# First attention: who counts the scores above the 32nd, ScalarE's sign pass or GpSimd's clamp with TensorE's row products

## What is computed

```python
scores = jnp.einsum('bthd,bghd->bhtg', Q, K) / np.sqrt(DH)     # 16 x 4 x 256 x 1601
topv, topi = jax.lax.top_k(scores, K_TOP)                       # K_TOP = 32
probs = jax.nn.softmax(topv, axis=-1)
attn = jnp.zeros_like(scores).at[bi, hi, ti, topi].set(probs)
c_t = jnp.einsum('btg,bgd->btd', attn.mean(axis=1), V)
```

## Time and profile before

| what | value |
|---|---|
| runs | 2945.46, 2946.61, 2954.35 us (median 2946.61) |
| span of the profiled execution | 2943.0 us, 3.6 us under the median run |
| first attention, from the first keep to the last | 1019.03 us, 127 slot intervals |
| one batch in the middle of it | 64.88 us, 8 slots |
| busy share in that batch | ACT 89%, PE 84%, DVE 82%, POOL 77% |

### The profile page before, as it was taken

How to read it: one execution, slowest core, us unless ns; L and a number is a source line. 1 busy time by engine, 2 the same in 40 slices (tenths; PEclk the granted TensorE clock), 3 DMA queues, 4 the chain that set the end, 5 groups by cost and what they waited for, 6 DMA issues and landing times. The chain is left out here.

```text
span 2943.0 us, 61087 instructions
## 1 busy us (share of the span) xinstructions
PE 2435.4 (83%) x19797; PEld 1266.0 (43%) x19797; DVE 2219.5 (75%) x8233; ACT 2102.0 (71%) x3547; POOL 1247.5 (42%) x1593
## 2 busy tenths in 40 slices
PE   7958888888888888668786589999999999999638
PEld 5735555555555555535422123333333333333337
DVE  8739878887887888446555989999999999994313
ACT  5759889888898988614322078888888888889325
POOL 1438777777777777613100502232222222200154
PEclk9979899989988998889898599999999999999669
DMA  8820000000000000091430224444344334330222
GB/s 241 266 76 12 13 15 13 14 13 13 17 20 13 15 13 13 8 308 36 60 118 32 79 43 100 101 102 101 90 95 101 87 92 94 94 64 2 59 92 67
DMA packets 163461, 205.77 MB, mean 70 GB/s; under 512 B 78588, under 2 KB 131106, under 8 KB 163126
## 3 DMA queue, kind: packets, MB, share of 16 engines
q1 hardware_dynamic: 152774, 161.80, 21.9%
q0 software_dynamic: 10352, 39.92, 4.0%
HBM read 135.19 MB, written 66.60 MB: 69 GB/s over the span
## 5 line engine op out<-in xcount | busy, mean ns | idle before, releaser
L2143 ACT ACTIVATE pb<-sps 128x512 f32<-128x512 f32 (+1 forms) x1664 | 891.9, 597 | 232.8 <-PE sps L2085 224.8
L2166 DVE TENSOR_REDUCE mx<-wps 128x2 f32<-128x802 f32 x1024 | 949.6, 988 | 49.8 <-PE wps L2058 35.0
L1076 DVE MAX8 cand<-sc 128x8 f32<-128x46 f32 (+1 forms) x4480 | 604.0, 199 | 138.3 <-issue 78.2
L2100 PE MATMUL ops<-pb,va 128*9 128x256 f32 x6656 | 516.4, 382 | 11.0 <-ACT ot L2149 7.2
L852 PE MATMUL scores<-ctxT,qT 97*128 97x512 f32 (+1 forms) x1024 | 437.2, 576 | 80.5 <-ACT sc L964 69.5
L852 PEld LDWEIGHTS scores<-ctxT,qT 97*128 97x128 f32 x1024 | 206.6, 212 | 318.4 <-issue 218.5
L1942 POOL COPY va<-XX 128x128 f32<-128x128 f32 (+1 forms) x208 | 49.9, 292 | 661.0 <-PE ops L2100 653.2
L735 POOL TENSOR_TENSOR prf<-sc,prf 128x1601 f32<-128x1601 f32 x64 | 229.7, 3589 | 127.0 <-ACT prf L971 127.0
L827 PE MATMUL misc<-diag,prs 128*128 128x128 f32 (+1 forms) x1664 | 238.0, 300 | 7.0 <-issue 6.1
L735 POOL TENSOR_TENSOR prs<-sc,prs 128x1601 f32<-128x1601 f32 x64 | 230.7, 3604 | 16.8 <-ACT prs L971 13.9
L2058 PE MATMUL wps<-FO,Y 56*128 56x401 bf16 x1024 | 187.8, 357 | 51.3 <-DVE mx L2166 36.4
(11 more groups left out here) (406 smaller groups left out, 3914.2 us busy)
## 6 DMA issues: line engine op xcount, KB each, us to landing
FO<-keys SPq DMA_DIRECT2D x392, 50.0 KB
XX<-keys SPq DMA_DIRECT2D x392, 50.0 KB
ctxn<-in_ctx_dram SPq DMA_DIRECT2D x32, 576.0 KB
keys<-kpb POOLq DMA_DIRECT2D x42, 400.2 KB, 3.7
toep<-kernpad SPq DMA_DIRECT2D x8, 2048.0 KB, 14.9
values<-s_vs SPq DMA_DIRECT2D x16, 832.0 KB, 6.0
XX<-values SPq DMA_DIRECT2D x16, 832.0 KB, 4.9
keysf<-s_kf SPq DMA_DIRECT2D x16, 800.5 KB, 3.8
```

Source lines behind the costliest of these rows:

```text
L1076: st.add(v.max(cand[s % 2][:, 8 + n:8 + n + 7 * NP + 1:NP], sc[s % 4][:, c:c + w]))
L2100: ins = t.matmul(ops[VW * i:VW * i + DH1 + 1, 0:S], va[par][0:kn(kt), kt, 4 * g + i, :], pb[(UNITS * g + 2 * kt + i % 2) % 8][0:kn(kt), i ...
L2143: nc.scalar.activation(pb[(UNITS * g + u) % 8][0:rows_, :, :], sps[(UNITS * g + u) % SB][0:rows_, :, :], ACT.Exp).then_inc(p_ready, 1)
L2166: v.tensor_reduce(mx4[:, q, h:h + 2, c], both, AX.X, ALU.max).then_inc(work_read, 1)
```

## The change

The sign pass leaves ACT, and `below32_of` leaves POOL. `keep_of` on POOL gets a clamp in front of the subtraction: the huge values in `pr` become 1 and the kept ones stay 0, written as bf16 to `side`. PE multiplies `side` with a column of -1 in four products of up to 401 columns into one row of PSUM, and adds the expected count with a fifth product. ACT sums that row of 401 into `doubts` (float; DVE loads its bits as an integer, positive where the float is positive).

```diff
+        COUNTED = -(-NK // 4)
-            st.link(g.memset(onecol[:, :], 1.0))
-            st.link(g.memset(plain[:, :], float(NK - 2 * TOPK)))
+            st.link(g.memset(onecol[:, :], -1.0))
+            st.link(g.memset(plain[0:P // 2, :], -3136.0))
+            st.link(g.memset(plain[P // 2:P, :], -(2.0 * (NK - TOPK) - 3136.0)))
...
-            def below32_of(s, j):
-
-                if not isinstance(j, int) or j >= 2:
-                    pool.wait_ge(sides_ready, j - 1)
-                pool.sem_inc(pool_passed, 1)
-                t32, e = top[:, s % 4, TOPK - 1:TOPK], slack[:, s % 2:s % 2 + 1]
-                st.link(g.tensor_scalar(e, t32, -1.0, t32, ALU.mult, ALU.max))
-                g.tensor_scalar(below32[:, s % 2:s % 2 + 1], e, 2.0 ** -22, t32, ALU.mult, ALU.subtract
-                                ).then_inc(below32_ready, 1)
...
             def keep_of(s, j):
 
                 pool.wait_ge(below_ready, j + 1)
+                if not isinstance(j, int) or j >= 2:
+                    pool.wait_ge(doubts_ready, j - 1)
+                st.link(g.tensor_scalar(side[s % 2][:, :], pr[s][:, :], 1.0, 0.0, ALU.min, ALU.max))
+                pool.sem_inc(side_ready, 1)
                 g.tensor_tensor(pr[s][:, :], sc[s % 4][:, :], pr[s][:, :], ALU.subtract).then_inc(kept_ready, 1)
...
-                    below32_of(s, j)
...
-                pe.wait_ge(sides_ready, j + 1)
+                pe.wait_ge(side_ready, j + 1)
                 if not isinstance(j, int) or j > 0:
                     pe.wait_ge(doubts_out, j)
-                t.matmul(dps[0:1, 0:1], sides[:, s % 2:s % 2 + 1], onecol[:, :], start=True, stop=False)
+                for c in range(0, NK, COUNTED):
+                    w = min(COUNTED, NK - c)
+                    t.matmul(dps[0:1, 0:w], onecol[:, :], side[s % 2][:, c:c + w], start=(c == 0), stop=False)
                 t.matmul(dps[0:1, 0:1], plain[:, :], onecol[:, :], start=False, stop=True).then_inc(doubts_ready, 1)
...
-            def side_of(s, j):
-
-                act.wait_ge(below32_ready, j + 1)
-                if not isinstance(j, int) or j >= 2:
-                    act.wait_ge(doubts_ready, j - 1)
-                s_.activation(side[s % 2][:, :], sc[s % 4][:, :], ACT.Sign, bias=below32[:, s % 2:s % 2 + 1],
-                              accum_out=sides[:, s % 2:s % 2 + 1]).then_inc(sides_ready, 1)
...
-                s_.copy(doubts[0:1, s % 2:s % 2 + 1], dps[0:1, 0:1]).then_inc(doubts_out, 1)
+                s_.activation(flags[0:1, :], dps[0:1, 0:COUNTED], ACT.Copy,
+                              accum_out=doubts[0:1, s % 2:s % 2 + 1]).then_inc(doubts_out, 1)
...
-                        side_of((s - 1) % NS, j - 1)
```

More of the change, by code:

```diff
@@ L583, in attention0_phase @@
         FEW = 8 + RANKS * NP
+        COUNTED = -(-NK // 4)
+        MOST = int(np.float32(P * NK).view(np.int32))
         cand = [sb(f"cand{i}", [P, 8 + 8 * NP]) for i in range(2)]
@@ L586, in attention0_phase @@
         side = [sb(f"side{i}", [P, NK], BF16) for i in range(2)]
-        sides = sb("sides", [P, 2])
-        onecol, plain = sb("onecol", [P, 1]), sb("plain", [P, 1])
-        doubts = sb("doubts", [1, 2], I32)
+        onecol, plain = sb("onecol", [P, 1], BF16), sb("plain", [P, 1], BF16)
+        flags, doubts = sb("flags", [1, COUNTED]), sb("doubts", [1, 2])
         cut, cutoff, negm = sb("cut", [P, NS]), sb("cutoff", [P, NS]), sb("negm", [P, NS])
-        slack, below32 = sb("slack", [P, 2]), sb("below32", [P, 2])
         den = sb("den", [P, NS])
@@ L605, in attention0_phase @@
         thr_ready, cut_ready, below_ready, kept_ready = sem("thr_ready"), sem("cut_ready"), sem("below_ready"), sem("kept_ready")
-        below32_ready, sides_ready, doubts_ready, doubts_out, settled = (
-            sem("below32_ready"), sem("sides_ready"), sem("doubts_ready"), sem("doubts_out"), sem("settled"))
+        side_ready, doubts_ready, doubts_out, settled = (
+            sem("side_ready"), sem("doubts_ready"), sem("doubts_out"), sem("settled"))
         exp_done, rden_ready, pair_done, diag_ready = sem("exp_done"), sem("rden_ready"), sem("pair_done"), sem("diag_ready")
@@ L1033, in _ @@
             below_of(B - 1, NS - 1, NS * B - 1)
-            side_of(NS - 1, NS * B - 1)
             doubts_of(NS - 1, NS * B - 1)
@@ L1067, in settle @@
                 dve.sem_inc(slot_begun, 1)
-                n = dve.value_load(doubts[0:1, s % 2:s % 2 + 1], min_val=0, max_val=2 * P * NK)
+                n = dve.value_load(doubts[0:1, s % 2:s % 2 + 1].bitcast(I32), min_val=0, max_val=MOST)
                 with dve.If(n > 0):
```

## The result

The changed kernel takes 3114.77 us (median of four runs, 3107.64 to 3120.32) against 2950.48 for the kernel before in the same comparison (four runs, 2945.46 to 2959.37): a ratio of 1.0544, 95% interval 1.0508 to 1.0579, so 5.4% slower. The forecast was 3068, slower, with a range of 2930 to 3200. The direction came as forecast, and so did the two main terms (the clamp in the loop, the hold of the cut); the size was 47 us short. The profiled execution took 3115.24, its span 3113.5.

What follows compares the result with a forecast made beforehand. A closed POOL-ACT loop of 5.98 us, not ACT's 89% busy share, bounds the slots. Slot terms sum to 1138.8 against 1019.0 (+119.8), plus 1.7 at the end: 3068 us, 4.1% slower, range 2930 to 3200.

Steps and rivals of the forecast that it cites:

- the clamp in the loop: POOL's new clamp stands between ACT's below and the subtraction, adding 1.52 + 0.20 us to the closed loop.
- the hold of the cut: POOL's cut chain, behind the subtraction, waits for DVE's pair addition: 1.9 us in odd slots with a pair.
- Plain slot: 7.70: Subtraction to subtraction without a held pair: the 5.98 us loop plus 1.72 for clamp and handover.
- The slower clamp: Rival: POOL's clamp takes longer than 1.52; at 2.5 us the kernel takes 3193 us, at 5.6 about 3590; chance 0.20.
- The pair addition moves into the subtraction: Odd steps: DVE's pair addition, ready at 4.70, meets POOL's subtraction, is held 2.3 us, then holds the cut chain.
- The rival in which nothing is held: Subtraction and pair addition go side by side; all slots cost 7.70 us, in all 2948 us; chance 0.18.
- the one in which the cut chain slips ahead: Rival: POOL's cut chain precedes the pair addition, only the diagonal is held; odd slot 8.9, some 3030 us; chance 0.08.
- Odd slot with a pair: 9.60: Odd-step slots: the plain 7.70 us plus 1.9 for the held cut chain, 63 times.
- The output rows: Odd step, s = 3: POOL's output rows take 3.1 us with the gap, 1.80 covered, so 1.3 stays, 15 times.
- PE's sums in steps 2 and 6: PE waits for the diagonal, then sums and counting end at 7.4 to 9.0 us against 7.70: excess 0.7, 31 times.
- In other steps the counting hides: Outside steps 2 and 6, PE's counting of the flag adds nothing; `side` comes 3.3 us after below, as the sign pass did.
- The time outside the phase: Outside first to last subtraction: only the last slot's clamp on the path to the end, +1.7 us.

Runs made afterwards that it cites:

- experiment 5: Changed kernel with the clamp over 64 of 1601 columns and the counting fed with zeros: 2926.39 us (measured once), phase 981.5.
- experiment 3: Changed kernel with a one-input MAX8 search in place of DVE's two-input pair addition: 3008.02 us (measured once), phase 1075.1.
- Experiment 2: Changed kernel with unused products on PE ahead of its wait for the clamp in steps 4 and 0: 3043.11 us (measured once), phase 1112.0.
- experiment 1: Changed kernel with the context sums moved ahead of the flag's counting in steps 0 and 4: 3062.92 us (measured once), phase 1119.7.

## Why the forecast was right in direction and short in size

The 127 slots after, by steps, against the terms of the sum:

| slots | forecast | measured mean | difference in all |
|---|---|---|---|
| odd with a pair, 63 | 9.60, step 3 10.9 | 9.25, step 3 10.50 | -22 |
| steps 2 and 6, 32 | 7.70 + 0.7 | 7.91 and 8.08 | -12 |
| steps 4 and 0, 31 | 7.70 | 9.35 and 9.94 | **+60** |
| the first | 7.70 | 10.63 | +3 |

Together +29: 1138.8 forecast, 1167.8 measured.

- *"Plain slot: 7.70."* Right. The clamp takes 1.53 (forecast 1.52) and hands over in 0.18 (0.20); the bare loop shows as 7.66 to 7.68, and experiment 5 shows that its whole length counts. The slower clamp falls as a rival. With it falls the estimate of 2.4 us from the Trainium skill's GPSIMD Engine Reference, "Elementwise — side-by-side cycle accounting": 0.96 ns an element was measured. I took its 1.8 cycles for a tight loop. The same section of the Trainium skill also has 1.03 cycles an element for a loop body with k ≤ 2, which at 1.2 GHz is an estimate of 0.86 ns. The 0.84 ns a column of experiment 5 agrees with that one.
- *"The pair addition moves into the subtraction."* Right, place and mechanism. The forecast had it ready 4.70 behind below and the subtraction from 3.43 to 7.00; the trace has 654.03 and 652.76 to 656.34, with below at 649.33: 4.70, and 3.43 to 7.01. The record of 3.98 answers the 4.2 forecast. The rival in which nothing is held falls with the trace, and so does the one in which the cut chain slips ahead, since it is the cut that is held; experiment 3 shows that the pair addition is the cause. The rule of the Trainium skill (SBUF — State Buffer, "Who interferes with whom"), that a VectorE instruction with two SBUF inputs contends with a GpSimd instruction that reads SBUF and that one with at most one, outside the 2-port modes, does not, agrees with 3.98 against 1.81. Whether the one-input instruction of the earlier trace rows was held for such a mode, no run here shows.
- *"Odd slot with a pair: 9.60."* 0.36 too much. I charged the length of a pair addition and a handover, 1.9. What is lost is the cut's delay, 1.76 - 0.20 = 1.56: only 1.67 of the addition remain when the subtraction ends, and the cut's own time runs within it.
- *"The output rows"*, 1.3: right, 10.58 - 9.24 = 1.34 in the median, 1.25 in the mean.
- *"PE's sums in steps 2 and 6"*: the 0.7 was about twice too much; over 7.67 they cost 0.24 and 0.41 in the mean.
- *"In other steps the counting hides."* This is the step that failed. The sum has the term at zero; it measures about 60 us, in steps 4 and 0. I compared when `side` comes (3.3 behind below) with when the sign pass delivered it and with when DVE's branch is due. I did not ask what stands behind the counting on PE, nor how long PE has then stood idle. In these two steps the counting stands ahead of the sums for which ACT waits before below. `side` itself is late in step 4 alone (4.68 behind below against 3.29, since POOL's output rows go first) and not in step 0 (3.36 against 3.35). What moved is PE: in step 4 shown above its scores end 1.19 ahead of below (674.30 and 675.49), where they ended 2.01 behind it (608.29 and 606.28). So PE, with little more work in longer slots, stands idle for 5 to 6 us. Behind that it runs at 1.2 GHz, so that the products take 1.50 instead of 0.85 and the sums, in the rows shown and in step 0 of that batch, 4.7 to 4.8 instead of 3.0. Experiment 2, which leaves the order and takes 55.8 us off the phase, shows that the clock is the cause; experiment 1 shows that the order lets it reach the loop in step 4. The Trainium skill (TensorE: Matmul & The Clock Gate, "What's actually happening") states that TensorE has these two levels and falls to the lower when idle; the windows at 0.60 and 1.00 agree.
- *The time outside the phase*: +1.7 forecast, +21.7 in these two profiles (1924.0 and 1945.7). In the eight experiments, none of which edits that part, it is 1929 to 1943. The profile of before lies 5 under this scatter and that of the changed kernel 3 over it, so these 20 us can't be put down to the change, and the forecast's 1.7 can't be tested by them.

So the 47 us between forecast and measurement are some 29 in the phase, of which the clock behind PE's wait accounts for more than all, and a scatter outside it. The 12.9 us a batch of the sign pass bought nothing that outweighs the clamp: as forecast, the closed loop holds ACT's below, but not the sign pass.

## What to carry to other kernels

Find the closed loop and sum it in one pass from an instruction to its next instance; a busy share of 89% on one engine (ACT) does not say that relieving it helps, and an operation put into a loop of two engines counts in full (1.53 + 0.18 us in 127 slots). When an operation moves others in time, look up what they now meet: here a two-input VectorE pass that came to overlap a GpSimd pass cost a wait for whatever was queued behind (1.57 us a slot). And when a wait on TensorE grows, price the work behind it at its duration at the lower clock, taken from a place in the trace where that clock was granted; if that work is waited for, move it ahead of the wait, or fill the wait.

## What was not expected of the hardware

- Behind a wait of 5 to 6 us on TensorE, work took half as long again and more (0.85 to 1.50, 3.0 to 4.7), and products of no use put into such waits made the whole kernel faster: 1.8% for the kernel before (ratio 0.9816), 2.3% for the changed one (3114.77 to 3043.11, the latter one run).
- Taking the held GpSimd instruction away passed the hold on to the next one: with the one-column pair gone, the diagonal took 2.18 instead of 0.62 in the median.
- The clamp of 128x1601 from f32 to bf16, with two steps, took as long as a plain cast of that shape: 1.53 against 1.52.
